# Memory attention over 64-token segments: half-height matmul pairs, another order of the steps, and a copy moved to GpSimd

## The chip, the cores and the metric

The kernel runs on one core of a Trainium2 chip. The metric is the device time of one execution in microseconds (us), the median of several runs. Engines are named as the profile names them: PE is TensorE (PEld its weight loads), DVE VectorE, ACT ScalarE, POOL GpSimd, SP SyncE.

## The reference

The program is four layers of attention and feed-forward blocks on 1024 tokens of width 256. The change touches the attention of the last layer alone. For each of 16 heads (width 128) it walks over 16 segments of 64 tokens:

```python
def step(carry, seg):
    mem, z = carry
    qq, kk, vv = seg
    sigma_q = elu(qq) + 1.0
    scores = where(causal_mask, einsum('bhsk,bhtk->bhst', qq, kk) / scale, -inf)
    att_dot = softmax(scores) @ vv
    att_mem = sigma_q @ mem / (sigma_q @ z)
    sigma_k = elu(kk) + 1.0
    delta = vv - sigma_k @ mem / (sigma_k @ z)
    mem_new = mem + einsum('bhsk,bhsv->bhkv', sigma_k, delta)
    z_new = z + sigma_k.sum(axis=-2, keepdims=True).transpose(0, 1, 3, 2)
    att = beta * att_mem + (1.0 - beta) * att_dot
    out = att.reshape(Bsz, SEG, H * DV) @ Wo
    return ((mem_new, z_new), out)
```

## The kernel before

`l3_attention` takes the heads two at a time (index `a` in 0, 1), in eight pairs: pair 0 is written out, pairs 1 to 7 are a hardware loop. Each engine has an order of its own, written out by hand, and the engines meet only at semaphores.

A pair has a first phase and 15 steps. In the first phase TensorE makes queries and keys (`projections(a)`, in four chunks), the values (`values`), the scores of all segments (`scores(a)`), and the keys transposed (`keys_by_token(a)`). ScalarE and VectorE make sigma of both (`queries_keys` and `sigma(j)`, j from 0 to 7), copy values and keys out of the banks, and start the softmax (`read_scores`, `largest`, `shift`, `exponential`, `total`, `normalize`). ScalarE's `place_keys(a)` copies the keys' sigma into `sg`, where queries and keys of a segment stand beside each other so that one matmul reads the memory for both.

Step n reads the memory for both heads (`read_memory`, line 2097), VectorE turns what was read into a delta (`delta`: a reciprocal, line 2368, and line 2371), TensorE adds it to the memory in its bank (`write_memory`, line 2087), and ScalarE copies the memory out (`mem_copy`, line 2234), for the next step's read. This is the chain that has to be walked 15 times. Between the reads and the writes of a step TensorE has one block of other work, the filler: `project_out` of the pair before (line 2020, steps 1 to 7), `turn_probs` (line 2108, steps 8 and 10), `local_attention` (line 2121, steps 9, 11, 12, 13), and `turn_reads` (line 2135, steps 14, 15 and behind the last). A tile of 128 tokens holds two segments, the even one in rows 0 to 63 and the odd one in rows 64 to 127; each of these matmuls uses all 128 rows, and the rows of the other segment count for nothing (zeros in `v`, `probs` and `turn`). `add_reads` (line 2378) adds the memory's part to the output of the pair; `dot_scale` (line 2248) has put the local part there before.

Three places are needed for the steps below:

```python
pe.matmul(k.bank[:, MEM + a, 0:W1], nkt[:, a, n // 2, n % 2, :], dr[:, a, n, 0:W1], start=False,
          stop=False, skip_group_check=True).then_inc(s["mem_ready"], 1)
last = pe.matmul(k.bank[:, 2 + c, at:at + S], v[:, t, a, o, :],
                 pt[:, a, t, o * S:(o + 1) * S], start=True, stop=True)
last = pe.matmul(k.bank[:, 2 * c + a, at:at + S], dr[:, a, n, 0:P], turn[:, HALF[1 - n % 2]],
                 start=True, stop=True)
```

## Time and profile before

| | |
|---|---|
| median of 3 runs | 2045.21 us (2043.0 to 2052.14) |
| the profiled run | 2052.14 us, its span 2050.4 us |
| busy in the span | PE 1785.6 (87%), DVE 1044.2 (51%), ACT 882.1 (43%), POOL 244.2 (12%) |
| `l3_attention`, first projection to last output projection | 1353.5 to 1929.8 us of the span |
| looped pairs start at (PE, line 2034) | 1428.7, 1499.4, 1568.7, 1639.4, 1708.7, 1780, 1850 us |

The page gives each engine's busy time, where in the span it is busy, the clock that TensorE was granted, and the costliest groups of instructions. What an engine waited for is not in the busy times; for that the timeline is read, one engine at a time, where each group shows the idle time before it and what ended it. Durations of matmuls overlap, so the time that one takes is read from the starts of groups.

### The profile page before, as it was taken

How to read it: one execution, taken by the hardware profiler on the slowest of the kernel's cores; microseconds unless marked ns; L12 is line 12 of the kernel's file. 1: busy time of each engine (PE TensorE's matmuls, PEld its weight loads, DVE VectorE, ACT ScalarE, POOL GpSimd, SP SyncE). 2: the span in 40 equal slices, each digit the busy share in tenths (PEclk: the TensorE clock that was granted, in tenths of full speed). 3: DMA queues.
4: the chain of work that ended last, by engine and by line, in shares of the span. 5: the costliest groups of instructions: out<-in, count | busy, mean ns of one | idle time of the engine just before them, and what ended most of it. 6: DMA issues, size and time to landing. Idle time of an engine off the chain costs nothing. (4 is left out here: it accounts for less than half of the span.)

```text
span 2050.4 us, 27324 instructions
## 1 busy us (share of the span) xinstructions
PE 1785.6 (87%) x9347; PEld 1447.8 (71%) x9347; DVE 1044.2 (51%) x2075; ACT 882.1 (43%) x1698; POOL 244.2 (12%) x237
## 2 busy tenths in 40 slices
PE   5988786987689999999877969969889989988898
PEld 4676544765568888887635758758888878878855
DVE  2266436234445555455565345554655565556466
ACT  3466324332244333433774343353444354344434
POOL 2010002212022222221101112220000000000000
PEclk8999996988789999999898979977999999999989
DMA  2000030110033433342100124220000000000100
GB/s 103 6 15 10 0 132 1 39 31 0 18 106 108 117 115 107 113 118 66 52 0 19 28 73 115 65 72 1 16 16 0 15 15 15 0 15 0 40 0 20
DMA packets 47074, 91.49 MB, mean 45 GB/s; under 512 B 7697, under 2 KB 24081, under 8 KB 46810
## 3 DMA queue, kind: packets, MB, share of 16 engines
q1 hardware_dynamic: 47026, 90.89, 14.7%
q8 instruction: 26, 0.43, 0.1%
q14 instruction: 22, 0.18, 0.0%
HBM read 89.52 MB, written 1.35 MB: 44 GB/s over the span
## 5 line engine op out<-in xcount | busy, mean ns | idle before, releaser
L438 PE MATMUL bank<-l1m_src_hi,l1m_w_hi 128*128 128x512 f32 x384 | 150.4, 392 | 7.5 <-DVE l1m_src_lo L507 7.5
L2234 ACT ACTIVATE l_mem<-bank 128x129 f32<-128x129 f32 x240 | 62.3, 279 | 217.1 <-PE bank L2087 216.3
L438 PE MATMUL bank<-l1m_src_hi,l1m_w_lo 128*128 128x512 f32 x384 | 150.1, 391 | 0.0
L438 PE MATMUL bank<-l1m_src_lo,l1m_w_hi 128*128 128x512 f32 x384 | 150.1, 391 | 0.0
L410 POOL TENSOR_TENSOR l1m_w_lo<-l1m_w,l1m_w_hi 128x512 fp32r<-128x512 f32 x96 | 104.8, 1109 | 325.5 <-ACT l1m_w_hi L475 325.5
L514 DVE TENSOR_TENSOR l1m_a<-l1m_s,bank 128x512 f32<-128x512 f32 x96 | 66.1, 688 | 116.6 <-ACT l1m_s L487 116.6
L491 ACT ACTIVATE l1m_a_hi<-l1m_a 128x512 fp32r<-128x512 f32 x96 | 60.7, 632 | 146.6 <-DVE l1m_a L520 146.6
L2368 DVE RECIPROCAL l_inv<-bank 128x1 f32<-128x1 f32 x240 | 39.2, 164 | 146.8 <-PE bank L2097 145.2
L2097 PE MATMUL bank<-l_mem,l_sg 128*128 128x129 f32 x480 | 94.4, 318 | 14.3
L2087 PE MATMUL bank<-l_dr,l_nkt 128*128 128x129 f32 x480 | 86.5, 302 | 21.7 <-issue 20.9
L528 DVE TENSOR_TENSOR l1m_a_lo<-l1m_a,l1m_a_hi 128x512 fp32r<-128x512 f32 x96 | 66.5, 692 | 70.8 <-ACT l1m_a_hi L491 70.8
L2097 PEld LDWEIGHTS bank<-l_mem,l_sg 128*128 128x128 f32 x480 | 69.4, 200 | 37.7 <-ACT l_mem L2234 37.4
L487 ACT ACTIVATE l1m_s<-bank 128x512 f32<-128x512 f32 x96 | 57.4, 598 | 88.0 <-PE bank L438 88.0
L438 PEld LDWEIGHTS bank<-l1m_src_hi,l1m_w_hi 128*128 128x128 f32 x384 | 72.6, 189 | 24.1 <-issue 9.1
L2087 PEld LDWEIGHTS bank<-l_dr,l_nkt 128*128 128x128 f32 x480 | 70.5, 205 | 25.7 <-issue 22.2
L2371 DVE SCALAR_TENSOR_TENSOR l_dr<-bank,l_inv,l_v 128x128 f32<-128x128 f32 x240 | 84.3, 351 | 8.5
L438 PEld LDWEIGHTS bank<-l1m_src_hi,l1m_w_lo 128*128 128x128 f32 x384 | 72.5, 189 | 15.3
L438 PEld LDWEIGHTS bank<-l1m_src_lo,l1m_w_hi 128*128 128x128 f32 x384 | 72.7, 189 | 15.1
L452 PE MATMUL bank<-l1m_a_hi,l1m_w_hi 128*128 128x512 f32 x192 | 74.8, 390 | 0.8 <-DVE l1m_a_lo L528 0.8
L452 PE MATMUL bank<-l1m_a_hi,l1m_w_lo 128*128 128x512 f32 x192 | 74.7, 389 | 0.0
L452 PE MATMUL bank<-l1m_a_lo,l1m_w_hi 128*128 128x512 f32 x192 | 74.7, 389 | 0.0
L2020 PE MATMUL bank<-h_modulated,l_wo 128*128 128x128 f32 x512 | 70.4, 289 | 1.3 <-DVE h_modulated L2378 1.3
(538 smaller groups left out, 4471.0 us busy)
## 6 DMA issues: line engine op xcount, KB each, us to landing
l1m_w<-in_l1f_win SPq DMA_DIRECT2D x48, 256.0 KB, 2.9
l1m_wr<-l1f_token_weights SPq DMA_DIRECT2D x32, 384.0 KB, 3.4
l1m_wr<-l1f_token_weights SPq DMA_DIRECT2D x32, 256.0 KB, 3.8
l_w<-in_l_w SPq DMA_DIRECT2D x9, 768.0 KB, 4.4
wmod<-in_wmod SPq DMA_DIRECT2D x4, 1536.0 KB, 9.8
l1m_w<-in_l1f_wout SPq DMA_DIRECT2D x48, 128.0 KB, 3.0
l1m_wr<-l1f_token_weights SPq DMA_DIRECT2D x32, 128.0 KB, 3.1
l2e_wr<-l2f_token_weights SPq DMA_DIRECT2D x16, 256.0 KB, 3.9
```

The source lines that it names most:

```text
L410: pool.tensor_tensor(w_lo[:, half, part], w[:, half, part], w_hi[:, half, part].bitcast(F32), ALU.subtract).then_inc(split_, 1)
L438: last = pe.matmul(k.bank[:, 2 * c + part, :], wq[:, half, at:at + P], xq[:, b, chunk(c)], start=(b == 0 and q == 0), stop=(b == DB - 1 an ...
L452: last = pe.matmul(k.bank[:, 4 + 2 * m + c, :], wq[:, half, at:at + P], aq[:, c, :], start=(first and q == 0 and not extra), stop=False, s ...
L487: act.activation(s[:, c, :], k.bank[:, 2 * c, :], ACT.Silu).then_inc(act_ready, 1)
L491: act.activation(a_hi[:, c, :], a[:, c, :], ACT.Identity).then_inc(hi_ready, 1)
L514: last = dve.tensor_tensor(a[:, c, :], s[:, c, :], k.bank[:, 2 * c + 1, :], ALU.mult)
L528: dve.tensor_tensor(a_lo[:, c, :], a[:, c, :], a_hi[:, c, :].bitcast(F32), ALU.subtract).then_inc(lo_ready, 1)
L2020: last = pe.matmul(k.bank[:, Y, m * P:(m + 1) * P], wo[:, j, tile(m)], att_by_row[:, :, j, :], start=(j == 0), stop=(j == H - 1))
L2087: pe.matmul(k.bank[:, MEM + a, 0:W1], nkt[:, a, n // 2, n % 2, :], dr[:, a, n, 0:W1], start=False, stop=False, skip_group_check=True).then ...
L2097: pe.matmul(k.bank[:, READ + a, 0:W1], sg[:, a, n // 2, at:at + 2, :], mem[:, a, n % 2, 0:W1], start=True, stop=True).then_inc(s["read_rea ...
L2234: act.activation(mem[:, a, (n + 1) % 2, 0:W1], k.bank[:, MEM + a, 0:W1], ACT.Identity).then_inc(s["mem_copied"], 1)
L2371: dve.scalar_tensor_tensor(dr[:, a, n, 0:P], k.bank[:, READ + a, 0:P], inv[:, a, n % 2:n % 2 + 1], v[:, n // 2, a, n % 2, :], ALU.mult, AL ...
```

## The change

It does five things in `l3_attention`, and nothing elsewhere.

- `local_attention` and `turn_reads` use 64 rows of each operand instead of 128, as pairs: the even segment from the upper rows into one bank, the odd one from the lower rows into another. `att_by_half`, `dot_scale` and `add_reads` follow: their columns are now every other 64. `add_reads` now comes in a piece of seven tiles and a last one of one tile, each as two instructions.
- Filler stands in two places of a step, before the writes (`before_write`) and after them (`after_write`). `local_attention(a)` is one block now.
- The last tile of `turn_reads` and its `add_reads` move into the next pair, behind its first projection chunk.
- The first phase is reordered: `values(1)` behind `scores(0)`; softmax pieces of VectorE move into the steps; the odd half of `keys_copy(0)` moves from ScalarE to VectorE; `keys_copy(1)` stands before the last `sigma`.
- `place_keys` is done by GpSimd, in four additions of zero a pair, and the first reads wait for half of it only.

The diff, cut to its core (indentation cut by twelve):

```diff
+    def place_keys(i, a, c):
+        pool.wait_ge(s["sigma_ready"], i * 8 + (4 * a + c + 1))
+        if a or c:
+            pool.wait_ge(s["keys_placed"], i * 4 + (2 * a + c))
+        pool.tensor_tensor(sg[:, a, 4 * c:4 * c + 4, 0::3, :], by_segment(keys[:, a, chunk(c)]),
+                           by_segment(k.zeros[:]), ALU.add).then_inc(s["keys_placed"], 1)
+    with pool.Fori(0, PAIRS) as i:
+        for a in range(HP):
+            for c in range(NCH):
+                place_keys(i, a, c)
...
+    def turn_reads(i, a, begin, end):
+        if begin == 0:
+            for o in range(2):
+                pe.wait_ge(s["dot_scaled" if a else "pt_copied"], i * 4 + (2 + o + 1))
+        if begin == LAST:
+            pe.wait_ge(s["reads_added"], i * 8 + (2 * a + 2))
+        for t in range(begin, end):
+            pe.wait_ge(s["delta_ready"], i * CHAIN + (HP * 2 * t + a + 1))
+            for o, half in enumerate((ODD, EVEN)):
+                last = pe.matmul(k.bank[:, 2 * a + o, t * S:(t + 1) * S], dr[half, a, 2 * t + o, 0:P],
+                                 turn[half, half], start=True, stop=True)
+        if end >= LAST:
+            last.then_inc(s["turned"], 1)
...
-                pe.wait_ge(s["sigma_ready"], i * 8 + 8)
-                pe.wait_ge(s["keys_placed"], i * HP + (a + 1))
+            if n in (1, NS // 2):
+                pe.wait_ge(s["sigma_ready"], i * 8 + (4 * a + 3 + n // (NS // 2)))
+                pe.wait_ge(s["keys_placed"], i * 4 + (2 * a + 1 + n // (NS // 2)))
...
-        def local_attention(a, c):
-            pe.wait_ge(s["pt_copied"], i * 4 + (2 * a + c + 1))
+        def local_attention(a):
+            pe.wait_ge(s["pt_copied"], i * 4 + (2 * a + 2))
             if a:
-                pe.wait_ge(s["dot_scaled"], i * 4 + (c + 1))
-            elif 2 + c == Y and not first:
+                pe.wait_ge(s["dot_scaled"], i * 4 + 2)
+            elif not first:
                 pe.wait_ge(s["x_added"], i)
-            for t in range(4 * c, 4 * c + 4):
-                for o in range(2):
-                    at = (t % 4) * P + o * S
-                    last = pe.matmul(k.bank[:, 2 + c, at:at + S], v[:, t, a, o, :],
-                                     pt[:, a, t, o * S:(o + 1) * S], start=True, stop=True)
+            for t in range(TT):
+                for o, half in enumerate(HALF):
+                    last = pe.matmul(k.bank[:, 2 + o, t * S:(t + 1) * S], v[half, t, a, o, :],
+                                     pt[half, a, t, half], start=True, stop=True)
             last.then_inc(s["dot_ready"], 1)
...
-        def turn_reads(a, c, segments):
-            if segments[0] == 0:
-                pe.wait_ge(s["pt_copied"], i * 4 + (2 + a + 1))
-            if segments[0] == 8:
-                pe.wait_ge(s["dot_scaled"], i * 4 + (2 + a + 1))
-            for n in segments:
-                if n:
-                    pe.wait_ge(s["delta_ready"], i * CHAIN + (HP * (n - 1) + a + 1))
-                at = (n % 8) * S
-                last = pe.matmul(k.bank[:, 2 * c + a, at:at + S], dr[:, a, n, 0:P], turn[:, HALF[1 - n % 2]],
-                                 start=True, stop=True)
-            if segments[-1] % 8 == 7:
-                last.then_inc(s["turned"], 1)
...
+        def before_write(n):
+            if n <= 6 and not first:
+                project_out(i, 5 * n - 5, 5 * n - 2)
+            if n == 7:
+                if not first:
+                    project_out(i, Y_PARTS - 2, Y_PARTS)
+                turn_probs(0, 0)
+            if n == 8:
+                local_attention(0)
+            if n == 9:
+                turn_probs(1, 0)
+            if n == 10:
+                turn_reads(i, 0, 0, 5)
+            if n == 11:
+                local_attention(1)
+            if n == 12:
+                turn_reads(i, 0, 5, 6)
+            if n == 13:
+                turn_reads(i, 1, 0, 6)
+            if n == 14:
+                turn_reads(i, 0, 6, LAST)
+                turn_reads(i, 1, 6, LAST)
+        def after_write(n):
+            if n <= 6 and not first:
+                project_out(i, 5 * n - 2, 5 * n)
+            if n == 7:
+                turn_probs(0, 1)
+            if n == 9:
+                turn_probs(1, 1)
         pe.wait_ge(s["w_split"], i * DB + DB)
-        projections(0)
-        values()
+        projections(0, (0,))
+        if not first:
+            for a in range(HP):
+                turn_reads(i - 1, a, LAST, TT)
+        projections(0, (1, 2, 3))
+        values(0)
         scores(0)
+        values(1)
         keys_by_token(0)
-        projections(1)
+        projections(1, range(4))
         keys_by_token(1)
         scores(1)
         for a in range(HP):
...
         for n in range(1, NS):
             for a in range(HP):
                 read_memory(n, a)
-            if n <= 7 and not first:
-                project_out(i, n - 1)
-            if n in (8, 10):
-                for c in range(NCH):
-                    turn_probs((n - 8) // 2, c)
-            if n in (9, 11):
-                local_attention(0, (n - 9) // 2)
-            if n in (12, 13):
-                local_attention(1, n - 12)
-            if n in (14, 15):
-                turn_reads(n - 14, 0, range(0, 8))
+            before_write(n)
             if n < NS - 1:
                 for a in range(HP):
                     write_memory(n, a)
-        for a in range(HP):
-            turn_reads(a, 1, range(8, NS - 1))
-        for a in range(HP):
-            turn_reads(a, 1, range(NS - 1, NS))
+                after_write(n)
     parts = [(b, hq, wq) for b in range(DB) for hq, wq in ((h_hi, w_hi), (h_hi, w_lo), (h_lo, w_hi))]
     pe.wait_ge(s["zeroed"], 1)
...
     pe.wait_ge(s["wo_in"], 16)
     with pe.Fori(1, PAIRS) as i:
         pair(i, False)
-    for part in range(len(Y_AT) - 1):
-        project_out(PAIRS, part)
+    for a in range(HP):
+        turn_reads(PAIRS - 1, a, LAST, TT)
+    project_out(PAIRS, 0, Y_PARTS)
...
-            if a == 0:
-                act.activation(nkt[ODD, a, :, 1, :], k.bank[ODD, at:at + 2, :].rearrange(
-                    "p n (t q) -> p (n t) q", q=P), ACT.Identity, scale=-1.0
-                    ).then_inc(s["kt_odd_copied"], 1)
-        def place_keys(a):
-            act.wait_ge(s["sigma_ready"], i * 8 + (4 * a + 2))
-            act.activation(sg[:, a, :, 0::3, :], by_segment(keys[:, a]), ACT.Identity
-                           ).then_inc(s["keys_placed"], 1)
...
-        def dot_scale(a, c):
-            act.wait_ge(s["dot_ready"], i * 4 + (2 * a + c + 1))
-            act.activation(att[:, a, chunk(c)], k.bank[:, 2 + c, :], ACT.Identity, scale=bt[:, 1, a:a + 1]
-                           ).then_inc(s["dot_scaled"], 1)
+        def dot_scale(a):
+            act.wait_ge(s["dot_ready"], i * HP + (a + 1))
+            for o in range(2):
+                act.activation(att_by_half[:, a, o], k.bank[:, 2 + o, :].rearrange("p (t q) -> p t q", q=S),
+                               ACT.Identity, scale=bt[:, 1, a:a + 1]).then_inc(s["dot_scaled"], 1)
         for j in range(4):
             queries_keys(j)
-        place_keys(0)
         values_copy(0)
+        exponential(0)
         values_copy(1)
-        exponential(0)
         keys_copy(0)
+        act.wait_ge(s["v_even_copied"], i * 2 + 1)
+        act.activation(dr[:, :, 0, 0:P], v[:, 0, :, 0, :], ACT.Identity, scale=-1.0
+                       ).then_inc(s["first_ready"], 1)
         for j in range(4, 8):
             queries_keys(j)
         keys_copy(1)
-        act.activation(dr[:, :, 0, 0:P], v[:, 0, :, 0, :], ACT.Identity, scale=-1.0
-                       ).then_inc(s["first_ready"], 1)
-        place_keys(1)
         for n in range(NS - 1):
             for a in range(HP):
                 mem_copy(n, a)
-            if n == 2:
+            if n in (2, 4) and not final:
+                high_part(i + 1, (n - 2) // 2)
+            if n == 5:
                 exponential(1)
-            if n in (3, 5) and not final:
-                high_part(i + 1, (n - 3) // 2)
-            if n in (8, 10):
+            if n in (7, 9):
                 for c in range(NCH):
-                    probs_copy((n - 8) // 2, c)
-            if n in (9, 11):
-                dot_scale(0, (n - 9) // 2)
-            if n in (12, 13):
-                dot_scale(1, n - 12)
+                    probs_copy((n - 7) // 2, c)
+            if n in (8, 11):
+                dot_scale((n - 8) // 3)
...
+    def add_reads(i, a, begin, end):
+        dve.wait_ge(s["turned"], i * 4 + ((3 if end == TT else 1) + a))
+        dve.wait_ge(s["dot_scaled"], i * 4 + 4)
+        for o in range(2):
+            rows = att_by_half[:, a, o, begin:end, :]
+            dve.scalar_tensor_tensor(rows, k.bank[:, 2 * a + o, begin * S:end * S].rearrange(
+                "p (t q) -> p t q", q=S), bt[:, 0, a:a + 1], rows, ALU.mult, ALU.add
+                ).then_inc(s["reads_added"], 1)
...
-        def add_reads(a, c):
-            dve.wait_ge(s["turned"], i * 4 + (2 * c + a + 1))
-            rows = att[:, a, chunk(c)]
-            dve.scalar_tensor_tensor(rows, k.bank[:, 2 * c + a, :], bt[:, 0, a:a + 1], rows, ALU.mult,
-                                     ALU.add).then_inc(s["reads_added"], 1)
-        for j in range(4):
+        for j in range(2):
+            sigma(j)
+            if j == 0 and not first:
+                for a in range(HP):
+                    add_reads(i - 1, a, LAST, TT)
+        for j in range(2, 4):
             sigma(j)
         if not first:
-            dve.wait_ge(s["reads_added"], i * 4)
+            dve.wait_ge(s["reads_added"], i * 8)
         step.link(dve, dve.tensor_copy(bt[:, 0, :], beta[:, bass.ds(i * HP, HP)]))
         step.link(dve, dve.tensor_scalar(bt[:, 1, :], bt[:, 0, :], -1.0, 1.0, ALU.mult, ALU.add))
         values_copy(0)
-        values_copy(1)
         read_scores(0)
         largest(0)
         shift(0)
-        for j in range(4, 6):
-            sigma(j)
-        total(0)
-        normalize(0, 0)
-        normalize(0, 1).then_inc(s["probs_ready"], 1)
-        for j in range(6, 8):
+        values_copy(1)
+        keys_copy(0)
+        for j in range(4, 7):
             sigma(j)
         keys_copy(1)
-        read_scores(1)
+        sigma(7)
         for n in range(1, NS):
             for a in range(HP):
                 delta(n, a)
             if n == 1:
+                read_scores(1)
+            if n == 2:
                 largest(1)
-            if n == 2:
+            if n == 3:
+                total(0)
+            if n == 4:
                 shift(1)
-            if n == 4:
+            if n == 5:
+                normalize(0, 0)
+            if n == 6:
+                normalize(0, 1).then_inc(s["probs_ready"], 1)
                 total(1)
-            if n == 5:
+            if n == 7:
+                if not first:
+                    add_projection(i)
                 normalize(1, 0)
-            if n == 6:
+            if n == 8:
                 normalize(1, 1).then_inc(s["probs_ready"], 1)
-            if n in (7, 9) and not final:
-                low_part(i + 1, (n - 7) // 2)
-            if n == 8 and not first:
-                add_projection(i)
-        dve.wait_ge(s["dot_scaled"], i * 4 + 4)
-        for c in range(NCH):
-            for a in range(HP):
-                add_reads(a, c)
+            if n in (9, 11) and not final:
+                low_part(i + 1, (n - 9) // 2)
+            if n == NS - 2:
+                add_reads(i, 0, 0, LAST)
+        add_reads(i, 1, 0, LAST)
...
```

## Rows read from the trace of the kernel before

**Rows 1.** Windows, two looped pairs: length; busy PE, PEld, DVE, ACT, POOL; clock; DMA
```profile
1428.70:1499.40 70.70, 64.62 (x511) 58.57 (x510) 40.49 (x106) 30.21 (x66) 0.00 (x0) 0.98 0.04 12
1499.40:1568.70 69.30, 63.07 (x511) 57.07 (x510) 40.50 (x106) 30.16 (x66) 0.00 (x0) 1.00 0.04 11
```

**Rows 2.** TensorE timeline, first phase: start, length, line, group, count, idle before
```profile
1519.95 1.09 PE L2057 MATMUL bank<-ident,l_keys 128*128 128x128 f32 x8 [1.51 <-DVE l_keys L2326]
1521.13 1.15 PE L2070 MATMUL bank<-l_qk 128*64 128x64 f32 x32
1525.76 0.46 PE L2087 MATMUL bank<-l_dr,l_nkt 128*128 128x129 f32 x2 [2.61 <-issue]
1526.05 1.02 PE L2097 MATMUL bank<-l_mem,l_sg 128*128 128x129 f32 x4
```

**Rows 3.** Timeline of VectorE in the same phase.
```profile
1517.58 0.43 DVE L2319 TENSOR_SCALAR l_e<-l_e 128x512 f32<-128x512 f32 x1 [3.28 <-ACT l_e L2206]
1524.43 1.23 DVE L2338 TENSOR_SCALAR l_nkt<-bank 64x1024 f32<-64x1024 f32 x1
```

**Rows 4.** Timeline of TensorE, starts of steps 3, 4, 8, 13 and 14.
```profile
1531.20 0.71 PE L2097 MATMUL bank<-l_mem,l_sg 128*128 128x129 f32 x4
1531.75 1.28 PE L2020 MATMUL bank<-h_modulated,l_wo 128*128 128x128 f32 x10
1532.87 0.61 PE L2087 MATMUL bank<-l_dr,l_nkt 128*128 128x129 f32 x4
1533.62 0.71 PE L2097 MATMUL bank<-l_mem,l_sg 128*128 128x129 f32 x4
1542.68 0.74 PE L2097 MATMUL bank<-l_mem,l_sg 128*128 128x129 f32 x4
1556.67 0.71 PE L2097 MATMUL bank<-l_mem,l_sg 128*128 128x129 f32 x4
1557.22 1.90 PE L2121 MATMUL bank<-l_qk,l_v 128*128 128x64 f32 x16
1558.96 0.66 PE L2087 MATMUL bank<-l_dr,l_nkt 128*128 128x129 f32 x4
1559.77 0.71 PE L2097 MATMUL bank<-l_mem,l_sg 128*128 128x129 f32 x4
```

**Rows 5.** Timeline of VectorE, step 13.
```profile
1557.40 0.35 DVE L2371 SCALAR_TENSOR_TENSOR l_dr<-bank,l_inv,l_v 128x128 f32<-128x128 f32 x1
1557.87 0.35 DVE L2371 SCALAR_TENSOR_TENSOR l_dr<-bank,l_inv,l_v 128x128 f32<-128x128 f32 x1
```

**Rows 6.** Timeline of ScalarE, step 13.
```profile
1559.43 0.50 ACT L2234 ACTIVATE l_mem<-bank 128x129 f32<-128x129 f32 x2 [2.01 <-PE bank L2087]
```

**Rows 7.** Groups by line and shape: busy us, mean ns; idle before.
```profile
L2243 ACT ACTIVATE l_qk<-bank 128x512 f32<-128x512 f32 x4 | 2.2, 598 | 0.0
L2229 ACT ACTIVATE l_sg<-l_keys 128x1024 f32<-128x1024 f32 x2 | 2.1, 1054 | 0.0
L2378 DVE SCALAR_TENSOR_TENSOR h_modulated<-bank,l_bt,h_modulated 128x512 f32<-128x512 f32 x5 | 3.7, 747 | 5.5 <-PE bank L2135 5.5
```

**Rows 8.** Timeline of TensorE, small matmuls of other layers.
```profile
556.34 1.95 PE L1431 MATMUL bank<-l1f_mask,ones 128*64 128x64 f32 x16
292.82 4.26 PE L980 MATMUL bank<-l0f_keys,l0f_q 64*128 64x64 f32 x32 [1.48 <-DVE l0f_q L1045]
```

**Rows 9.** The windows view, stretches that show the clock.
```profile
1388.30:1402.00 13.70, 12.90 (x42) 10.16 (x43) 8.02 (x26) 4.55 (x13) 0.00 (x0) 0.50 0.01 2
1456.00:1459.00 3.00, 3.00 (x16) 2.91 (x16) 1.46 (x4) 0.19 (x1) 0.00 (x0) 0.58 0.00 0
292.80:297.00 4.20, 4.18 (x32) 4.08 (x32) 0.00 (x0) 0.00 (x0) 0.00 (x0) 0.87 1.01 415
556.30:558.20 1.90, 1.90 (x18) 1.79 (x17) 0.00 (x0) 0.00 (x0) 0.00 (x0) 0.50 0.00 0
```

**Rows 10.** Groups by line and shape, GpSimd.
```profile
L410 POOL TENSOR_TENSOR l1m_w_lo<-l1m_w,l1m_w_hi 128x512 fp32r<-128x512 f32 x48 | 61.8, 1288 | 42.1 <-ACT l1m_w_hi L475 42.1
```

41 lines of the change are left out of this document (20 added, 21 removed).

## Prediction, before the changed kernel was run

> **What bounds the kernel now.** The profile's chain of waits is of no use here: it stops at the layer norm behind the changed function. I read the windows first. The function runs from 1353.5 us on: eight pairs of heads, of which the seven looped ones take 69.3 or 70.7 us each, with TensorE busy 91% and VectorE and ScalarE 58% and 44% [rows 1]. So TensorE's own order of work bounds it, and only less work on TensorE or fewer holes in it can pay. I cut the pair that starts at 1499.39 into three parts, by the starts of TensorE's groups. A "record" is one matmul instruction; a float32 matmul leaves two.
>
> First phase (projections up to the first memory read): 1499.39 to 1526.05, 26.66 us. TensorE stands still twice. It waits 1.51 us for the keys of the second head [rows 2]: ScalarE reached that head's first projection late, so VectorE began its sigma at 1517.58 after 3.28 us without work [rows 3]. Then 2.61 us at the second `write_memory(0)` [rows 2]. The view says "issue", but the code waits for `keys_copy(1)`, which VectorE runs from 1524.43 to 1525.66, and the write starts at 1525.76: it is this copy, queued behind softmax work and four sigmas.
>
> Steps 1 to 7: 1526.05 to 1542.68, 16.63 us. A step with ten filler records takes 2.42 us (1531.20 to 1533.62): 0.55 of reads, 1.12 of filler, 0.75 of writes and of waiting for the memory copy [rows 4]. Steps 8 to 15 with the tail: 1542.68 to 1568.68, 26.0 us. Here a step is 0.55 + 1.74 + 0.81 = 3.1 us (1556.67 to 1559.77), and the tail behind the last read runs 48 more records. 128 of the records of this part are the matmuls that the change halves, at 0.109 us each (1.74/16).
>
> The latency under a step, measured from its first read: VectorE's first delta instruction starts at +0.73 and ends at +1.08, the second ends at +1.55 [rows 4, 5]. From a write to the start of the memory copy it is 0.47, and both copies take 0.50 [rows 4, 6].
>
> **Part by part.**
> *64-row pairs.* Each full-height matmul (half of whose rows multiply zeros) becomes half-height; the count of instructions stays at 128 records a pair. So all depends on whether the upper and the lower half run side by side. No row shows row halves side by side. The nearest rows: 16 records of 64-column matmuls in one column half took 1.95 us, 0.122 each at half clock, so 0.061 at full clock [rows 8, 9]; the scores, whose two matmuls go to different column halves, take 1.15/32 = 0.036 [rows 2]. Sharing the array thus took 0.59 of the time. Half-height records that all lie in one row half took 4.26/32 = 0.133 at clock 0.87, no gain [rows 8, 9]. By the first ratio, the nearest, a record of the new kind takes 0.109 x 0.59 = 0.064; I take 0.066. Bounds: 0.036 (the scores' row) and 0.109 (no gain); I hold 0.054 for the practical low end, half of today's. Going over to the scores shows no gap in TensorE's rows [rows 2]; I charge 0.1 for each of eight blocks as a margin.
>
> The Trainium skill ("TensorE: Matmul & The Clock Gate", section on LDWEIGHTS) says that a weight load takes as long as its columns, 107 ns for 128, whatever its rows; the 0.109 agrees. By that rule alone each half costs what the whole did, and this is the first rival below. The same skill ("TensorEngine Tiling (Array Packing)", Key Properties) says that tiles load and multiply in parallel, and that a change of tiling drains the array.
>
> *Steps 8 to 15, new order.* I add for each step 0.55 of reads, the block, and 0.78 for write and copy; a light step is held by the latency to 2.05. Step 8: 0.55 + a wait of 0.4 for the second probability copy (it now follows a transposition placed behind the write; a copy is 0.60 [rows 7]) + 32 x 0.066 + 0.1 + 0.78 = 3.95. Step 9: 2.26. Step 10: 0.55 + 0.75 wait for the same kind of copies + 20 records 1.42 + 0.78 = 3.5. Step 11: 3.55. Step 12: 2.05. Step 13: 24 records, 3.0. Step 14: 2.1. Step 15: 0.55. Sum 21.0, against 26.0.
>
> *Steps 1 to 7.* The same 32 projections, 3 before the writes and 2 behind. The second head's delta holds the write to +1.6, the two behind it end at +2.26, by when both copies are done: 2.26 us. Six steps 13.6, the seventh (two projections, transposition on both sides, and VectorE 0.36 late from the softmax work moved into step 6) 2.7. Sum 16.2, against 16.6. Splitting the filler is worth next to nothing here, since five projections nearly covered the latency already.
>
> *First phase.* The odd-half key copy and both `place_keys` leave ScalarE, some 1.05 us each [rows 7]; with values(1) behind scores(0) the softmax hides under matmuls. The 1.51 goes: by my count sigma for the second keys is done 0.6 us before its projections end. Late next is ScalarE's last query copy, which holds scores(1) about 0.5, about what today's small waits take. The 2.61 goes too: `total` and `normalize` leave this queue and `keys_copy(1)` moves ahead of the last sigma. Added: eight left-over records, 0.63, behind the next pair's first projection chunk. The second head's wait for `reads_added` on the bank: VectorE has the last step's two `add_reads` (1.4 us for seven eighths of the columns at 0.75 each [rows 7]) before the last delta and two more behind it, so that they end 5.4 us after step 14 began, while TensorE is there at 4.3. I charge 1.15. Queued behind that wait are all later projections, and VectorE's first sigma. 26.66 - 1.51 - 2.61 + 0.63 + 1.15 = 24.3.
>
> *GpSimd.* Four additions of 128x512 a pair at 1.29 us [rows 10], 5.2 in 61 us, on an engine without other work here. The second head's first half is placed some 2 us before the read that needs it, the later halves by step 8; nothing waits even at double the price. `SP`'s load of the next weights waits for the same projections as before and still lands ahead of the split, now in steps 2 and 4. What I can't see is whether VectorE slows beside it: a bound from nothing up to a doubling of the 5.2 us, half of it exposed: 2.6 a pair, 20 in all. I take none, since sigma and the additions overlap only in part.
> The Trainium skill ("GPSIMD Engine Reference", Specifications) speaks against this edit: GpSimd shares its memory interfaces with VectorE, with contention when VectorE has two inputs in SBUF, as sigma has. No run here shows it. By it the sum would be toward 2000.
>
> *The clock.* In four of the seven loop pairs the clock dips right behind the 2.61 us wait (0.58 in 1456 to 1459) and such a pair takes 70.7 instead of 69.3 [rows 1, 9]. Without the wait I drop these 1.4 us, 5.6 in all.
>
> **Sum.** A looped pair: 24.3 + 16.2 + 21.0 = 61.5, against 69.3: 7.8. Six such, 47. The clock, 5.6. Pair 0 (no projections to fill, its steps 1 to 7 at half clock now [rows 9] and, I assume, later): 2.3 + 5.2 = 7.5. The last pair keeps its tail exposed: 5. Together 65 us. The profiled run took 2052.1 (span 2050.4), the median of three is 2045.2; the rest of the program is untouched, so I take the 65 from the median: **1980 us**.
>
> **Rivals.**
> *The halves don't run side by side.* 1024 records x 0.043 = 44 back: 2024. For it: the 64-row rows at 0.133. Against: these never offer the other half anything to do, and column halves do share.
> *VectorE late.* Its queue decides at the pair boundary and in steps 6 and 7. Were the waits of 2.85 us a pair that I charge (0.4 + 0.75 + 0.55 + 1.15) to double and steps 5 to 7 to lose 0.6, it would cost 3.4 x 7.6 = 26: 2006. VectorE would be busy some 43 of 62 us (40.5 today [rows 1], 1.2 for the odd keys, about 1 for more pieces), so it is order, not load.
> *Clock lost: the slower side.* Half-height matmuls and light steps (9, 12, 14) leave TensorE doing less. In pair 0 the unfilled steps ran at clock 0.50 throughout, with records covering 94% of the time, and the clock came back only with fillers [rows 9]. The dip cost 1.4 us for 3 us at 0.58, that is 1.26 us of clock: 1.1 for each. If 20 us of a pair ran at 0.50, 10 x 1.1 = 11, over 7.6 pairs 84: 1980 + 84 = 2064. It outweighs the gain from 15.5 us a pair on. Against it: today's 64-wide blocks and the scores leave the clock of such a pair at 1.00 [rows 1], and no two light steps adjoin.
> *It does nothing:* only if the waits that go are replaced one for one and the halves don't overlap; a part of the second and first rival together, about 2045.
>
> **Chances and range.** Forecast 0.68 (1955 to 2000), halves apart 0.12, VectorE late 0.08, clock 0.08, nothing 0.04. Records at 0.054 give 12 less, no waits at all another 20: 1955 at the low end; the high end takes in the rival at 2024. A measurement of this kernel tells about 0.5% from no change. Faster by more than that 0.88, within it 0.04, slower 0.08.
>
> **What would show it.** Right: 32 records of `local_attention` in about 2.2 us (3.5 if the halves are apart); no stretch of 2.6 us before the second write; pairs of 61 to 62 us; clock 1.00 from the first step on; a wait of about 1 us at the left-over matmuls; the first half of VectorE's sigma still 0.43. Wrong: a clock under 0.9 over whole pairs, sigma longer beside GpSimd, or blocks whose entry costs several tenths each.

## The result and the profile after

The changed kernel takes 1981.3 us (median of four runs, 1980.88 to 1981.94) against 2048.07 us before (four runs now, 2043.0 to 2052.14). The ratio is 0.9675, its 95% interval 0.965 to 0.9701: 66.8 us, or 3.3%, less. The profiled run took 1981.94 us with a span of 1980.1, so the two spans differ by 70.3.

The windows view of the changed kernel, first over all eight pairs, then over one looped pair, then over steps 1 to 7 of pair 0. Its columns are those of [rows 1].

```profile
1352.90:1859.70 506.80, 485.38 (x4064) 414.95 (x4064) 352.97 (x874) 222.29 (x502) 45.19 (x32) 0.99 0.04 11
1475.90:1537.70 61.80, 59.63 (x510) 51.19 (x509) 44.40 (x111) 27.98 (x63) 5.66 (x4) 1.00 0.04 13
1377.70:1393.10 15.40, 13.37 (x65) 9.10 (x65) 12.65 (x39) 6.09 (x19) 0.00 (x0) 1.00 0.02 6
```

TensorE is now busy 96% of a looped pair, against 91% in [rows 1]; it still sets the time. A looped pair starts every 61.76 us where it was 69.3 or 70.7 (the first of them takes 62.0), and the clock is 1.00 in pairs 1 to 6. The first pair's unfilled steps, which stood at clock 0.50 [rows 9], now run at 1.00. VectorE has gained work (44.4 us against 40.5) and GpSimd has some.

Where the 70 us are, by the starts of TensorE's groups in the two traces:

| part | before, us | after, us | less |
|---|---|---|---|
| ahead of the function | 1353.5 | 1352.9 | 0.6 |
| pair 0, start to start | 75.2 | 61.0 | 14.2 |
| pairs 1 to 6 | 419.9 | 370.8 | 49.1 |
| last pair, to the first output projection behind it | 72.2 | 65.1 | 7.2 |
| those output projections | 9.0 | 10.0 | -1.0 |
| the rest | 120.6 | 120.3 | 0.3 |

The output projections behind the last pair got slower: the windows view has them at clock 0.82 before and 0.72 after.

And inside a looped pair (before: the one from 1499.39; after: the one from 1475.93):

| part of a pair | before | forecast | after |
|---|---|---|---|
| first phase | 26.66 | 24.3 | 23.93 |
| steps 1 to 7 | 16.63 | 16.2 | 16.80 |
| steps 8 to 15 and tail | 26.0 | 21.0 | 21.03 |

TensorE's timeline of the changed kernel (start, length, line, group, count, idle before it and what ended it): first one step with fillers, which answers to the step from 1531.20 in [rows 4], then the two blocks of step 8 and step 10, then the pair's end with the left-over block.

```profile
1447.57 0.61 PE L2124 MATMUL bank<-l_mem,l_sg 128*128 128x129 f32 x4
1448.02 0.83 PE L2035 MATMUL bank<-h_modulated,l_wo 128*128 128x128 f32 x6
1448.68 0.87 PE L2114 MATMUL bank<-l_dr,l_nkt 128*128 128x129 f32 x4
1449.39 0.61 PE L2035 MATMUL bank<-h_modulated,l_wo 128*128 128x128 f32 x4
1449.84 0.61 PE L2124 MATMUL bank<-l_mem,l_sg 128*128 128x129 f32 x4
...
1454.90 0.61 PE L2124 MATMUL bank<-l_mem,l_sg 128*128 128x129 f32 x4
1455.98 2.00 PE L2146 MATMUL bank<-l_qk,l_v 64*128 64x64 f32 x32 [0.46 <-ACT l_qk L2267]
1457.91 0.71 PE L2114 MATMUL bank<-l_dr,l_nkt 128*128 128x129 f32 x4
...
1462.25 1.33 PE L2050 MATMUL bank<-l_turn,l_dr 64*128 64x64 f32 x20 [0.51 <-ACT l_qk L2267]
...
1475.10 0.85 PE L2124 MATMUL bank<-l_mem,l_sg 128*128 128x129 f32 x4
1475.93 0.49 PE L2064 MATMUL bank<-l_h_hi,l_w_hi 128*128 128x512 f32 x1
...
1477.52 0.90 PE L2050 MATMUL bank<-l_turn,l_dr 64*128 64x64 f32 x8
1478.34 0.50 PE L2064 MATMUL bank<-l_h_hi,l_w_hi 128*128 128x512 f32 x1
```

The filler of a step is now in two places, and the step takes 2.27 us, not 2.42. The block of 32 half-height records runs from 1455.98 to 1457.91: 1.93 us, 0.060 a record, against 0.109 in [rows 4]. The price of entering such a block does not lie in it but in its neighbours, and full-height blocks in the same places (the first experiment) show it: in step 11 the reads ahead of the block take 0.64 and the writes behind it 0.86, where those take 0.55 and 0.81. Two waits of about half a microsecond stand ahead of the blocks of steps 8 and 10. The left-over block shows no idle time, but its eight records take 0.82 where 0.060 each would be 0.5, so about 0.3 of waiting is in it.

VectorE's timeline of the same pair (same columns), two places:

```profile
1482.59 1.56 DVE L2358 SCALAR_TENSOR_TENSOR l_sg<-l_qk,l_e 128x512 f32<-128x512 f32 x1
...
1499.96 0.69 DVE L2358 SCALAR_TENSOR_TENSOR l_sg<-l_qk,l_e 128x512 f32<-128x512 f32 x1
1500.68 0.17 DVE L2400 RECIPROCAL l_inv<-bank 128x1 f32<-128x1 f32 x1
```

GpSimd's timeline:

```profile
1482.09 1.52 POOL L2016 TENSOR_TENSOR l_sg<-l_keys,zeros 128x512 f32<-128x512 f32 x1 [1.22 <-DVE l_keys L2358]
1494.08 1.55 POOL L2016 TENSOR_TENSOR l_sg<-l_keys,zeros 128x512 f32<-128x512 f32 x1 [10.47 <-DVE l_keys L2358]
```

Both lines over the whole run (shortest, middle and longest ns, first and last start):

```profile
L2358 DVE SCALAR_TENSOR_TENSOR l_sg<-l_qk,l_e x32: 691/1129/1665, 1360.5 to 1808.8; 128x512 f32<-128x512 f32 x32
L2016 POOL TENSOR_TENSOR l_sg<-l_keys,zeros x32: 1288/1314/1552, 1357.8 to 1805.2; 128x512 f32<-128x512 f32 x32
```

The same sigma instruction takes 0.69 us alone and 1.56 beside GpSimd's addition; the middle of 1129 ns lies between the two, since half of the 32 are of each kind. In each looped pair three of the eight sigmas meet an addition, and take 1.56, 1.57 and 1.65 us. This was the cost that the forecast bounded and then set to nothing.

### The profile page after: what moved, and what is told of

Its sections match the earlier page's. It is cut to its first block and busy times, and to the rows that moved or that the text cites. A ratio compares the mean times of both kernels' runs of the same rounds, so it can differ in the third digit from the quotient of the medians.

```text
span 1980.1 us, 27498 instructions
## 1 busy us (share of the span) xinstructions
PE 1745.5 (88%) x9347; PEld 1388.1 (70%) x9347; DVE 1074.3 (54%) x2115; ACT 864.0 (44%) x1674; POOL 289.2 (15%) x269
## 5 line engine op out<-in xcount | busy, mean ns | idle before, releaser
L2258 ACT ACTIVATE l_mem<-bank 128x129 f32<-128x129 f32 x240 | 65.1, 279 | 195.4 <-PE bank L2114 194.7
L2016 POOL TENSOR_TENSOR l_sg<-l_keys,zeros 128x512 f32<-128x512 f32 x32 | 45.2, 1412 | 415.2 <-DVE l_keys L2358 415.2
L2114 PE MATMUL bank<-l_dr,l_nkt 128*128 128x129 f32 x480 | 101.4, 310 | 3.9 <-DVE l_dr L2403 1.9
L2124 PE MATMUL bank<-l_mem,l_sg 128*128 128x129 f32 x480 | 85.7, 294 | 5.5
L2124 PEld LDWEIGHTS bank<-l_mem,l_sg 128*128 128x128 f32 x480 | 65.1, 190 | 18.9 <-ACT l_mem L2258 16.7
L2035 PE MATMUL bank<-h_modulated,l_wo 128*128 128x128 f32 x512 | 74.8, 282 | 0.6 <-DVE h_modulated L2342 0.6
```

The costliest lines, as they stand in the source:

```text
L2035: last = pe.matmul(k.bank[:, Y, m * P:(m + 1) * P], wo[:, j, tile(m)], att_by_row[:, :, j, :], start=(j == 0), stop=(j == H - 1))
L2124: pe.matmul(k.bank[:, READ + a, 0:W1], sg[:, a, n // 2, at:at + 2, :], mem[:, a, n % 2, 0:W1], start=True, stop=True).then_inc(s["read_rea ...
L2258: act.activation(mem[:, a, (n + 1) % 2, 0:W1], k.bank[:, MEM + a, 0:W1], ACT.Identity).then_inc(s["mem_copied"], 1)
```

## The experiments

The part ahead of the function starts TensorE's first projection at 1344.9 to 1354.0 us from one kernel's profile to the next, though nothing there differs. So beside each median I give the period, the time from the start of one looped pair to the next (from the third pair on, where the second differs), which repeats within 0.1 us in most kernels, and weigh theories by it. Ratios are to the kernel before on the same chip. The changed kernel's period is 61.76 and its median 1981.3.

**Full-height matmuls again.** Both kinds get all 128 rows back; order and count stay.

```diff
-    last = pe.matmul(..., v[half, t, a, o, :], pt[half, a, t, half], start=True, stop=True)
+    last = pe.matmul(..., v[:, t, a, o, :], pt[:, a, t, half], start=True, stop=True)
-    last = pe.matmul(..., dr[half, a, 2 * t + o, 0:P], turn[half, half], start=True, stop=True)
+    last = pe.matmul(..., dr[:, a, 2 * t + o, 0:P], turn[:, half], start=True, stop=True)
```

> The changed kernel, but local_attention and turn_reads use all 128 rows again, in the same places, banks and order; each pair of heads keeps its 128 records in these blocks. Theory (the halves run side by side and that is most of the gain): a block of 32 records takes 3.5 us instead of 1.9, 128 records x 0.049 us = 6.3 us a pair, less what falls into waits, so 1981 + 45 = about 2026 us. Rival (the gain comes from the order and the waits that went): under 10 us slower than the changed kernel.

Measured: 2020.19 us, ratio 0.9864 (0.9829 to 0.9898), period 66.95, that is 5.19 more. From the reads of step 8 to those of step 15 it takes 25.33 us instead of 20.20. The block of step 8, from TensorE's timeline of this kernel:

```profile
1520.08 3.79 PE L2146 MATMUL bank<-l_qk,l_v 128*128 128x64 f32 x32 [0.46 <-ACT l_qk L2267]
1523.70 0.66 PE L2114 MATMUL bank<-l_dr,l_nkt 128*128 128x129 f32 x4
```

3.62 us from start to start, 0.113 a record. Same order, same wait, same records: the half height alone is worth 39 us (2020.19 against 1981.3), where 45 was expected.

**Half-height matmuls, one half after the other.** Does the gain come from two halves that run side by side, or from each being smaller? The two loops of `local_attention` change places, so that eight even-half matmuls precede eight odd-half ones.

```diff
-    for t in range(TT):
-        for o, half in enumerate(HALF):
+    for o, half in enumerate(HALF):
+        for t in range(TT):
```

> The changed kernel, but local_attention issues all its upper-half matmuls first and all its lower-half ones after, so neighbours in TensorE's order use the same half of the rows; the instructions are the same ones. Theory (the gain is overlap of neighbours in different halves): the block of 32 records goes back to about 3.5 us from 1.93, as with full height; two blocks a pair, 1.55 each, 3.1 us a pair and eight pairs: 1981 + 24 = 2005 us. Rival (a half-height record is cheaper by itself): the block stays at about 2 us and the time at 1981.

Measured: 2041.93 us (ten runs, 2030.2 to 2062.29), ratio 0.9957 (0.9929 to 0.9984). That is 37 us more than expected, and its runs lie further apart than those of any other kernel here. Windows of this kernel:

```profile
1454.70:1463.70 9.00, 8.91 (x72) 8.02 (x71) 7.20 (x25) 3.45 (x11) 0.00 (x0) 1.00 0.01 2
1468.90:1474.50 5.60, 5.27 (x40) 5.07 (x40) 2.75 (x9) 2.91 (x7) 0.00 (x0) 0.71 0.01 3
1479.60:1484.70 5.10, 5.10 (x21) 4.23 (x20) 1.09 (x5) 2.27 (x6) 0.00 (x0) 0.50 0.00 0
1590.00:1624.00 34.00, 32.45 (x264) 28.91 (x264) 19.88 (x66) 12.60 (x35) 0.00 (x0) 1.00 0.00 0
```

TensorE's timeline, the two blocks of one pair:

```profile
1464.77 3.39 PE L2146 MATMUL bank<-l_qk,l_v 64*128 64x64 f32 x32 [0.46 <-ACT l_qk L2267]
1468.08 0.71 PE L2114 MATMUL bank<-l_dr,l_nkt 128*128 128x129 f32 x4
...
1476.03 3.64 PE L2146 MATMUL bank<-l_qk,l_v 64*128 64x64 f32 x32
1479.61 1.23 PE L2114 MATMUL bank<-l_dr,l_nkt 128*128 128x129 f32 x4
```

The block takes 3.31 us, 0.103 a record: a half-height matmul by itself costs nearly what a full-height one does. So the halves overlap when they alternate, and the gain is the overlap. In two of the eight pairs (the one that holds the window from 1590 to 1624 is one) the stretch from step 8 to step 15 took 22.98 us, 2.78 more than in the changed kernel, close to the expected 3.1. In the other six the clock fell behind a block, to 0.71 and then 0.50, and that stretch took 26.9 to 29.8. TensorE hardly stood still there: it was busy 5.27 of 5.60 us and 5.10 of 5.10. The experiment before has full-height blocks of 3.62 us in the same places and keeps the clock at 1.00 over a whole looped pair. What differs is that each of the two long blocks works with one half of the rows at a time; that this is the cause was not tested further, and why two pairs escape is open.

**Filler in one place.** All five projections before the write, and the second transpositions before it too; `after_write` is gone.

```diff
     def before_write(n):
         if n <= 6 and not first:
-            project_out(i, 5 * n - 5, 5 * n - 2)
+            project_out(i, 5 * n - 5, 5 * n)
...
-    after_write(n)
```

> The changed kernel, but all filler stands before the writes again, none behind them. Theory (splitting is worth little): a step with five projections takes 2.42 instead of 2.27 us, six of them 0.9 us a pair more, and the two waits of 0.5 us for copies of probabilities shrink, 0.9 less: 1975 to 1987 us. Rival (the split is what makes the steps short): over 1995 us.

Measured: 1986.82 us, ratio 0.9698 (0.9663 to 0.9733), period 62.53, 0.77 more. Steps 1 to 7 take 17.46 instead of 16.80, steps 8 to 15 0.12 more. The two waits that were expected to shrink did not: steps 8 and 10 take 3.99 and 3.42, against 3.86 and 3.24. TensorE's timeline of one step:

```profile
1448.16 0.71 PE L2124 MATMUL bank<-l_mem,l_sg 128*128 128x129 f32 x4
1448.71 1.28 PE L2035 MATMUL bank<-h_modulated,l_wo 128*128 128x128 f32 x10
1449.82 0.61 PE L2114 MATMUL bank<-l_dr,l_nkt 128*128 128x129 f32 x4
1450.58 0.71 PE L2124 MATMUL bank<-l_mem,l_sg 128*128 128x129 f32 x4
```

The step is 2.42 us, that of [rows 4] to the hundredth, and the split takes 0.15 from each of five. Worth 5 to 6 us in all, with the medians 5.5 apart and the intervals overlapping.

**Softmax early again.** VectorE has the softmax of the first head ahead of the second keys' copy, as before the change.

```diff
-    for j in range(4, 7):
+    for j in range(4, 6):
+        sigma(j)
+    total(0)
+    normalize(0, 0)
+    normalize(0, 1).then_inc(s["probs_ready"], 1)
+    for j in range(6, 8):
         sigma(j)
     keys_copy(1)
-    sigma(7)
```

> The changed kernel, but VectorE sums and normalizes the first head's softmax before sigma 6 and 7 again and copies the second keys last, as in the kernel before. Theory (the 2.6 us wait was this queue): the second write of step 0 waits again, 2 to 2.6 us a pair, and the clock dips behind it, in pair 0 for its steps without filler too (15.4 us now, about 18 then): 1981 + 16 to 28 = about 2003 us. Rival (the wait went because ScalarE is free of place_keys and the odd keys): under 6 us more than the changed kernel.

Measured: 2012.95 us, ratio 0.9818 (0.9783 to 0.9852), periods 65.55 in the mean, 3.8 more. That is 32 us above the changed kernel, where 16 to 28 was expected: the first phase takes 2.9 to 3.2 us more in every looped pair, and the clock's dip behind it adds to step 1. TensorE's timeline, pair 0:

```profile
1376.82 0.39 PE L2114 MATMUL bank<-l_dr,l_nkt 128*128 128x129 f32 x2
1380.24 0.46 PE L2114 MATMUL bank<-l_dr,l_nkt 128*128 128x129 f32 x2 [3.04 <-issue]
```

Two windows around it:

```profile
1377.00:1381.00 4.00, 0.89 (x6) 0.53 (x5) 3.08 (x6) 0.54 (x2) 0.00 (x0) 0.97 0.19 76
1381.00:1397.00 16.00, 15.63 (x49) 12.01 (x50) 8.77 (x29) 5.35 (x16) 0.00 (x0) 0.50 0.01 2
```

The wait ahead of the second `write_memory(0)` is back, and behind it the clock stands at 0.50 for 16 us of pair 0, with TensorE busy 15.63 of them. In the changed kernel, without that wait, the same steps run at 1.00 with TensorE busy 13.37 of 15.40 us, and take 15.46 us, not 19.43. So in these two kernels the unfilled steps did not lower a clock that was up, nor raise one that was down.

**The kernel before with the late softmax alone.** The same edit from the other side, on the kernel before: nothing else of the change.

```diff
-    for j in range(4, 6):
-        sigma(j)
-    total(0)
-    normalize(0, 0)
-    normalize(0, 1).then_inc(s["probs_ready"], 1)
-    for j in range(6, 8):
+    for j in range(4, 7):
         sigma(j)
     keys_copy(1)
-    read_scores(1)
+    sigma(7)
```

`read_scores(1)` and `largest(1)` go to step 1, `total(0)` to 3, `normalize(0)` to 4 and 5, the second head's to 6 to 8.

> The kernel before with one part of the change alone: VectorE copies the second keys before its last sigma, and the first head's sums and normalizing move into the steps. ScalarE still places the keys, matmuls are full height. Theory (the 2.61 us wait was VectorE's queue): the wait goes, also the clock's dip behind it (0.7 us a pair on average, 3 us in pair 0): 3.3 us a pair, 27 us off the kernel before, about 2023 us. Rival (ScalarE's work is as late, its keys_copy and place_keys end only there): under 10 us off.

Measured: 2014.91 us, ratio 0.9813 (0.9789 to 0.9837): 37 us less, from the order of one queue, where 27 was expected. The profiles differ by 36.6, of which 3.1 lie ahead of the function and behind it, where nothing was changed; so the order is worth about 33 us, half of what the whole change takes off the function. TensorE's timeline of pair 0:

```profile
1374.83 1.09 PE L2057 MATMUL bank<-ident,l_keys 128*128 128x128 f32 x8 [1.50 <-DVE l_keys L2326]
...
1377.64 0.61 PE L2087 MATMUL bank<-l_dr,l_nkt 128*128 128x129 f32 x4
1378.53 0.68 PE L2097 MATMUL bank<-l_mem,l_sg 128*128 128x129 f32 x4 [0.29 <-ACT l_mem L2234]
```

A window of its steps:

```profile
1380.00:1400.00 20.00, 18.24 (x101) 13.39 (x100) 15.77 (x49) 8.49 (x24) 0.00 (x0) 1.00 0.00 1
```

The 1.50 wait stays; ScalarE's queue is the old one. The two writes follow each other: four records in one group, with no wait ahead of the second. The period is 66.74, 3.25 below the mean of before, as expected (3.3). Pair 0 loses 8.3 us, its steps running at 1.00, and that was not expected.

**ScalarE places the keys.** GpSimd's loop goes; ScalarE copies the keys behind the first four `queries_keys` and behind `keys_copy(1)`, the first reads wait for the whole placement, and everything else of the change stays.

```diff
-    with pool.Fori(0, PAIRS) as i:
-        for a in range(HP):
-            for c in range(NCH):
-                place_keys(i, a, c)
...
+    def place_keys(a):
+        act.wait_ge(s["sigma_ready"], i * 8 + (4 * a + 2))
+        act.activation(sg[:, a, :, 0::3, :], by_segment(keys[:, a]), ACT.Identity
+                       ).then_inc(s["keys_placed"], 1)
```

> The changed kernel, but ScalarE places the keys again (two copies of 1.05 us a pair, where they stood before). Theory (the move to GpSimd is worth something although sigma is slower beside it): all of VectorE's sigma take 0.69 us again, but ScalarE's second copy stands before its first memory copy and costs about 1 us a pair: 1981 + 8 = 1989 us. Rival (contention costs more than the copy): the three sigma of a pair that took 1.6 instead of 0.69 us were exposed, and the time falls by up to 2.6 us a pair, toward 1965 us.

Measured: 1977.43 us (1968.13 to 1980.78), ratio 0.964 (0.9597 to 0.9683). The interval overlaps that of the changed kernel, so the medians don't tell them apart; the trace does. From the third pair on the period is 61.18 to 61.31, some 0.5 less. Both sigma lines of this kernel (ns as above):

```profile
L2353 DVE SCALAR_TENSOR_TENSOR l_keys<-l_qk,l_e x32: 691/693/695, 1358.2 to 1801.0; 128x512 f32<-128x512 f32 x32
L2353 DVE SCALAR_TENSOR_TENSOR l_sg<-l_qk,l_e x32: 691/693/693, 1361.5 to 1805.2; 128x512 f32<-128x512 f32 x32
```

All 64 take 0.69 us; step 1 takes 2.37 us, not 2.66, and the first phase about 0.2 less. My expectation had the wrong sign: this part of the change costs 0.5 us a pair. The Trainium skill ("GPSIMD Engine Reference", Specifications) says that GpSimd and VectorE contend when VectorE's instruction has two inputs in SBUF, or is in a performance mode that uses two ports. For sigma, which has two such inputs, the trace of the changed kernel agrees, 1.56 against 0.69.

**GpSimd later.** Its additions wait for a later sigma, so that they meet other instructions of VectorE.

```diff
-    pool.wait_ge(s["sigma_ready"], i * 8 + (4 * a + c + 1))
+    pool.wait_ge(s["sigma_ready"], i * 8 + (4 if a == 0 else 5 + c))
```

> The changed kernel, but GpSimd's two additions for the first head wait until all four sigma of that head are done, so they run beside VectorE's copies out of the banks and its softmax pieces; the second head's are as they were. Theory (VectorE slows only where both its inputs are in SBUF): sigma of the first head 0.69 us each again, the copy out of a bank beside it stays 1.23 us, the second head's two slow sigma stay 1.6; the first head's delay was hidden, so 1981 within 2 us. Rival (any VectorE work beside GpSimd slows): the bank copies and scores grow and the time rises over 1985 us.

Measured: 1980.92 us, ratio 0.9677 (0.9647 to 0.9706), period 61.76: no gain. VectorE's timeline:

```profile
1480.68 1.28 DVE L2417 TENSOR_SCALAR l_bt<-l_bt 128x2 f32<-128x2 f32 x1
1482.08 1.23 DVE L2364 COPY l_v<-bank 64x1024 f32<-64x1024 f32 x1
```

GpSimd's timeline:

```profile
1480.65 2.65 POOL L2016 TENSOR_TENSOR l_sg<-l_keys,zeros 128x512 f32<-128x512 f32 x2 [48.84 <-DVE l_sg L2358]
```

The first head's sigma are back at 0.69. Now an instruction of 128x2 elements takes 1.28 us where it took 0.17. The copy out of a PSUM bank is not touched: it takes 1.23, as in [rows 3], while GpSimd's second addition runs. The instruction caught has one input, in SBUF, so it is not the case of two inputs; whether it is the skill's other case, the mode with two ports, no trace here tells. In the collisions of the changed kernel's looped pairs sigma ends 0.54 to 0.56 us behind GpSimd's addition (1484.15 behind 1483.61, for one), and the small one here ends at 1481.96, when the first of GpSimd's two is about done (half of 2.65 behind 1480.65). That looks like an instruction held until GpSimd's ends, not like one running slowly; no run was made for this alone.

**Half of a block on half of its data.** `local_attention` waits for the first probability copy, and for the second only at its middle; `local_attention(1)` moves to step 10 and `turn_reads` to 11, with `dot_scale` in 8 and 10.

```diff
-    pe.wait_ge(s["pt_copied"], i * 4 + (2 * a + 2))
+    pe.wait_ge(s["pt_copied"], i * 4 + (2 * a + 1))
...
     for t in range(TT):
+        if t == TT // 2:
+            pe.wait_ge(s["pt_copied"], i * 4 + (2 * a + 2))
```

> The changed kernel, but local_attention waits for the second copy of probabilities only in its middle, and steps 10 and 11 change places, so that turn_reads comes a step after the copies that free its banks. Theory (the two waits of 0.46 and 0.51 us a pair lie on TensorE's path): both go, 0.9 us a pair, 1981 - 7 = 1974 us. Rival (something else, such as ScalarE's memory copy behind them, is as late): under 2 us of gain.

Measured: 1969.84 us, ratio 0.9613 (0.9575 to 0.965), period 60.73, 1.03 less, where 0.9 was expected. TensorE's timeline, step 8:

```profile
1453.39 0.61 PE L2124 MATMUL bank<-l_mem,l_sg 128*128 128x129 f32 x4
1453.97 2.00 PE L2148 MATMUL bank<-l_qk,l_v 64*128 64x64 f32 x32
1455.91 0.71 PE L2114 MATMUL bank<-l_dr,l_nkt 128*128 128x129 f32 x4
```

No wait ahead of the block and none inside: 1.94 us for its 32 records. The 0.46 and 0.51 of the changed kernel were real losses, and both are gone (0.97 of the 1.03).

**Both: ScalarE places, waits split.** The two edits together, with `turn_reads(i, 1, ...)` spread over steps 12 and 13.

```diff
         if n == 12:
             turn_reads(i, 0, 5, 6)
+            turn_reads(i, 1, 0, 2)
         if n == 13:
-            turn_reads(i, 1, 0, 6)
+            turn_reads(i, 1, 2, 6)
```

> Changed kernel with three things together: ScalarE places the keys (0.55 us a pair less in the trace of that run), the waits for probabilities split and steps 10 and 11 exchanged (0.9 less expected), and eight records of turn_reads moved from step 13 into step 12, which the memory's chain holds at 2.0 us anyway (0.4 less expected). If these are independent: 1.85 us a pair, 1981 - 15 = 1966 us. If ScalarE, which has the placing and the copies, becomes late: 1970 us or more.

Measured: 1966.88 us (1964.44 to 1968.27), ratio 0.9602 (0.9572 to 0.9632), period 59.89. The window of one pair:

```profile
1472.60:1532.50 59.90, 58.61 (x509) 50.99 (x508) 41.77 (x111) 29.67 (x65) 0.00 (x0) 1.00 0.05 13
```

TensorE is busy 98%. The gains add up: 0.19 in the first phase and 0.29 in step 1, as with ScalarE alone, 1.03 as with the split waits, and 0.36 from the spread block (steps 12 and 13 take 4.85 us here and 5.21 with the split waits alone) make the 1.87 found. At 14.4 us below the changed kernel this is the fastest version by its period; its median's interval overlaps that of the split waits alone.

**Left-over reads at once.** The last tile's `turn_reads` and `add_reads` go back to the pair's end; nothing is carried over.

```diff
     projections(0, (0,))
-    if not first:
-        for a in range(HP):
-            turn_reads(i - 1, a, LAST, TT)
-    projections(0, (1, 2, 3))
...
+    for a in range(HP):
+        turn_reads(i, a, LAST, TT)
```

> The changed kernel, but the last tile of turn_reads and its add_reads stand at the end of their own pair instead of behind the next pair's first projection chunk. Theory (the move hides VectorE's two add_reads and the last delta): TensorE waits at the pair boundary about 2 us, the time from the last reads to the end of the second head's add_reads (2.7 us after the last read starts, minus 0.8 us of reads), 8 pairs: 1981 + 14 = 1995 us. Rival (the wait is hidden by slack later in the first phase, or costs the clock too): under 5 us, or over 25 us.

Measured: 1998.85 us, ratio 0.9743 (0.9726 to 0.976), period 64.74, 2.98 more. TensorE's timeline, the pair's end:

```profile
1475.09 0.85 PE L2124 MATMUL bank<-l_mem,l_sg 128*128 128x129 f32 x4
1476.33 0.44 PE L2050 MATMUL bank<-l_turn,l_dr 64*128 64x64 f32 x4 [0.39 <-DVE l_dr L2399]
1477.88 0.44 PE L2050 MATMUL bank<-l_turn,l_dr 64*128 64x64 f32 x4 [1.11 <-DVE h_modulated L2338]
```

Windows of the three microseconds from the first projection on, in pair 1 and in pair 2, and a line of VectorE's timeline a little later:

```profile
1414.95:1418.00 3.05, 3.05 (x15) 2.55 (x14) 1.06 (x4) 1.09 (x2) 0.00 (x0) 1.00 0.02 5
1478.35:1481.40 3.05, 3.05 (x7) 2.50 (x8) 0.47 (x2) 0.09 (x1) 0.00 (x0) 0.50 0.00 0
```

```profile
1483.56 1.29 DVE L2347 TENSOR_SCALAR l_e<-l_e 128x512 f32<-128x512 f32 x1 [0.36 <-ACT l_e L2236]
```

From the last read to the next projection it is now 3.26 us, not 0.83. The waits of 0.39 and 1.11 are the pair's last delta and VectorE's `add_reads`; the carried-over block had hidden both under one projection chunk. The first phase is 24.5 us, not 23.93, though it lost the left-over block. That is the clock: in every pair from the third on it stands at 0.50 to 0.58 for three microseconds behind these waits, and the 24 records of the first projections take 7.13 us instead of 5.80. The second pair shows the same phase without the dip, 23.14 us, though its VectorE meets GpSimd no less (1.56 and 1.67 us). The first of these two is the first half of a sigma, an instruction with one input that takes 0.43 otherwise (1.29 in the line above). The undone parts sum to 5.2 + 0.8 + 3.8 + 3.0 - 0.5 = 12.3 us a pair, more than the 8.2 gained over the mean period before (69.99): they lean on each other. The tail's waits, for instance, lay under 48 records before.

## Why the prediction was right, point by point

*What bounds the kernel.* Right. Every gain was one of TensorE's holes, of its records or of its clock, and 96% busy is what is left.

*64-row pairs.* Right, and the argument from column halves held for row halves: 0.060 a record against the forecast 0.066 (32 records in 1.93, forecast 2.2 with the entry). The margin of 0.1 for each block's entry was near what it costs: 0.09 in the reads ahead and 0.05 in the writes behind, against full-height blocks in the same place. A half that runs alone costs 0.103. The rule of the Trainium skill ("TensorE: Matmul & The Clock Gate", section on LDWEIGHTS), that a weight load takes its columns whatever its rows, agrees with that 0.103; taken alone it misses the 0.060 of two halves that alternate. The first rival priced this at 44 us; full height cost 39.

*Steps 8 to 15.* 21.03 against 21.0, but from terms that cancel. The blocks came out cheaper, and step 10's wait was 0.51 instead of 0.75 (3.24 against 3.5). Against that, step 13 took 3.22 against 3.0 and the end 0.83 against 0.55, since the reads there take 0.88 and 0.83 where I charged 0.55 throughout. Only 0.1 of it comes with the half height: at full height these reads take 0.79 and 0.72. That reads could be slow was not in the rows I used: those were read in steps with a long filler ahead.

*Steps 1 to 7.* 16.80 against 16.2: the one part that was forecast shorter and came out longer. The six steps of 2.26 were right for five (2.27) and wrong for the first, 2.66. The rows above show why: GpSimd has delayed VectorE's queue, so that `sigma(7)` runs from 1499.96 to 1500.65, and the first delta, queued behind it, begins at 1500.68, 0.82 behind the read (1499.86). The experiment with ScalarE has 0.53 there and a step of 2.37. The seventh took 2.80 against 2.7. "Splitting the filler is worth next to nothing" was mis-sized: it is 0.15 on five steps, since five projections in one block left the writes 0.15 late.

*First phase.* 23.93 against 24.3, again two errors that cancel. The wait at the left-over block, which I charged with 1.15, is about 0.3: the block of eight records takes 0.82 us with its wait, and eight records alone would be 0.5. VectorE's `add_reads` for both was 1.27, not 1.4, and it ended 4.8 us behind the start of step 14, not 5.4. Against that stand the sigma delay, some 0.2 here, and 0.3 that I had not charged: the first projections take 5.80 us with the left-over block between them, not 5.56, and the values in two parts 5.94, not 5.84. That the two waits of 1.51 and 2.61 would go was right: the experiment that puts the softmax back restores the second one, the one with ScalarE's old order keeps the first.

*GpSimd.* Here the step failed. I bounded the cost from nothing to 2.6 a pair and took nothing, because the overlap was partial. Sigma stretched from 0.69 to 1.56 where it met GpSimd, and 0.5 us a pair of that lies on the path: 4 us in all. The row for it is sigma's 1.56 us. The warning of the Trainium skill ("GPSIMD Engine Reference", Specifications) held in sign; the 2000 us that the prediction set beside it did not. Sigma longer beside GpSimd was named as a sign of being wrong, and it came; the total came right all the same, since the cost is small beside the gains.

*The clock.* The size per dip was right and the count too: with the wait gone no looped pair dips. The mis-sized term is pair 0. I assumed its unfilled steps would stay at half clock and gave it 7.5; it lost 14.2. Steps 1 to 7 took 15.46 against 18.70 before, at clock 1.00; that is 3.2 of the 6.7 missed. The first phase lost 4.0 where I had 2.3, and steps 8 to 15 lost 6.9 where I had 5.2, part of them at a lowered clock before. The experiments with the softmax early and late say that what had put it at half was the wait ahead of them (2.61 us), not their own lightness.

*Sum.* 61.76 against 61.5 a looped pair; 49.1 against 51.2 for six pairs with the clock; 14.2 against 7.5 for the first; 7.2 against 5 for the last, plus its share of the clock. The profiles differ by 70.3 where I said 65, the medians of the runs by 66.8. So the 1980 that was met within 1.3 us owes something to luck: misses of several microseconds, in pair 0 most of all, went against each other and against a kernel before whose median came out 3 us higher than the 2045.2 that I started from. The low end of the range does not follow from its terms: 1980 less 12 and 20 is 1948, not 1955.

*The rivals.* The halves don't overlap: refuted (0.060 a record against 0.113, first experiment). VectorE late: its waits shrank instead; but it did slow beside GpSimd. Clock lost: not in the changed kernel, and yet the mechanism exists. The second experiment shows it in six of eight pairs, at 2042 us, when half-height records no longer overlap. The argument against it, that 64-wide blocks keep the clock, was drawn from blocks that fill all rows; it would not have protected a version with the loops the other way.

## What to carry to other kernels

Before making matmuls cheaper, look for the engine whose queue holds the copy that a write waits for: moving one softmax behind it took, by itself, 37 us off the kernel before, where the whole change takes 67, and it also kept the clock up for the steps behind. The clock belongs to the price of a wait: those at a pair's end, put back, cost 1.3 us of slower records behind them in six pairs. The gain from half-height matmuls came from their alternating between the halves, so the loop over halves belongs inside. When work moves to GpSimd, price the VectorE instructions that will meet it, small ones too.
